# Taking 934 clears, and the waits for them, out from between GpSimd's indirect DMAs

## The chip, the cores and the metric

The kernel runs on one core of one Trainium2 chip. A core has five engines that run their own instruction streams: TensorE (PE), VectorE (DVE), ScalarE (ACT), GpSimd (POOL) and SyncE (SP). They meet only through semaphores. The metric is device time in microseconds (us) of one execution, as the median of the runs.

## The reference

Four graph layers, each followed by a layer norm, work on 100,000 nodes of 32 numbers and 25,000 edges that are sorted by `dst`. Cut to what matters:

```
x = norm(x + scatter_add(dst, message0(x[src], edge_weight, edge_attr_3)))      # layer 0
x = norm(x + mean of x and three hops of  segment_sum(w * x[src], dst))          # layer 1
x = norm(x + maximum(segment_max(mlp(x[src], x[dst], edge_attr_32), dst), x))    # layer 2
x = norm(x + (x + sum of attention messages over edges, by dst) @ W1 + b1)       # layer 3
```

Only nodes that are a `dst` get messages. The other nodes are norms and products of their own row alone. So the kernel keeps one row per edge for the `dst` side, and does the nodes in big chunks beside it.

## The kernel before

**Layout.** The 25,000 edges are padded to 25,088 and laid out as 128 partitions by T = 196 columns. A tile such as `A_dst` is [128, 196, 32]: one row of 32 numbers for each edge. Rows that are picked by an index come by an indirect DMA of one column: 128 indices, 128 rows. GpSimd issues them all, 1054 in the executed path, and nothing else issues one. The columns fall in 7 chunks of 28 (`GATHER_CHUNK`).

**GpSimd's stream, in order.** What it does is one straight line, written out by hand:

- 56 gathers of `x[src]` into `A_src` and 28 of `x[dst]` into `A_dst` (`in_x`). Here a helper `keep` paces them against VectorE's histogram. Nothing is cleared in front of them.
- 56 gathers from `pos_table` into `out_short` (columns of positions), 140 from `x_pos` into `A_src` (rows with the position appended), and 168 from `x` into `A_dst`. `x_pos` is a table that SyncE stores in 14 pieces; GpSimd waits for all of them (`x_stored`).
- the hops of layer 1: 60 gathers (`A_msg` from `table`, by `nxt_i`), 24 scatters to `edge_sums`, 22 gathers (by `idx_next`), 12 scatters, 22 gathers, 24 scatters, and 22 scatters from `A_tmp`. Each group waits for a table or for sums that VectorE makes out of the group before. VectorE does the node chunks (line 1495, line 2001 and others on `work`) between the hops, in an order that is fixed in its own stream.
- layer 2: 112 gathers (`work` from `table`), 16 for each of 7 windows; after each window VectorE moves rows into place with predicated copies (lines 2249 and 2253) and feeds the edge pipeline of TensorE and ScalarE.
- layer 3: 112 gathers (`A_msg` from `table`), again 16 for each of 7 windows, and then 196 scatters to `out` (line 880). The scatters come in 8 pieces of 20, six times 28, and 8 columns. Piece i waits for `final_ready` to reach i + 1, which VectorE's last multiplication of that piece (`A_dst<-A_dst,std`, line 1484) raises.

**The clear.** The helper `pause` (line 736 holds its memset) clears `gtmp[0:64]`, 64x64 numbers that nothing reads afterwards, raises the semaphore `cleared`, and makes GpSimd wait until that has arrived. It stands in front of 934 of the 1054 indirect DMAs. The other 120 go out one behind the other: the first 84 and the last 36 scatters to `out` (`if i < 6` leaves out pieces 6 and 7). Line 746 is the DMA in `gather`, lines 823 and 829 are those of the hops, line 880 is the scatter to `out`.

**VectorE's helpers.** Line 1484 is every elementwise operation of two tensors, line 1488 and line 1489 those of a tensor and scalars, line 1495 every reduction, line 1583 the running sums column by column (one scan for each of 32 features).

Of the kernel before, what the change touches and what calls it, by code (L numbers as in the profile page):

```python
# [10 lines left out]
T = -(-N_EDGES // P)  # L11
# [10 lines left out]
HEADS, HF = 2, 64  # L22
# [16 lines left out]
SLOTS_IN_WINDOW = 16  # L39
# [9 lines left out]
GATHER_CHUNK = 28  # L49
# [29 lines left out]
DST_FIRST = 1  # L79
# [9 lines left out]
def gnn_kernel(nc, x, src, dst, r_feat, rel, turned_attr, edge_weight, w1, b1, w2, b2,  # L89
# [12 lines left out]
    with ExitStack() as ctx:  # L102
# [3 lines left out]
        def sem(name):  # L106
            return ctx.enter_context(nc.semaphore(name))
# [5 lines left out]
        pos_table = dram("pos_table", (HI * P, 1))  # L113
# [157 lines left out]
        n_bank, seam_taken = sem("n_bank"), sem("seam_taken")  # L271
        n_var, n_std, n_z, n_zsq, n_out = sem("n_var"), sem("n_std"), sem("n_z"), sem("n_zsq"), sem("n_out")
        n_stored = [sem(f"n_stored_{s}") for s in range(SLOTS)]
        cleared = sem("cleared")
        mlp_in, maxima_taken = sem("mlp_in"), sem("maxima_taken")
        e_cat, e_turned, e_catT = sem("e_cat"), sem("e_turned"), sem("e_catT")
        e_h, e_hT, e_v, e_vused = sem("e_h"), sem("e_hT"), sem("e_v"), sem("e_vused")
# [419 lines left out]
        def _(pool):  # L697
# [32 lines left out]

            node_limit, edge_limit = pool.to_reg(N_NODES - 1), pool.to_reg(E_PAD - 1)

            def pause(tile):

                issued["cleared"] += 1
                pool.memset(tile, 0.0).then_inc(cleared, 1)  # L736
                pool.wait_ge(cleared, issued["cleared"])

            def gather(column, of, idx, limit, done, columns=range(T), keep=None, cleared_tile=None):

                for t in columns:
                    if keep:
                        keep()
                    if cleared_tile is not None:
                        pause(cleared_tile)
                    pool.indirect_dma_start(  # L746
                        out=column(t), out_offset=None, in_=of,
                        in_offset=bass.IndirectOffsetOnAxis(ap=idx[:, t:t + 1], axis=0),
                        bounds_check=limit, oob_is_err=False).then_inc(done(t), 16)

            pool.wait_ge(loaded_src, 48)
            pool.wait_ge(pads_ready, 2)
            issued = {"hist": 0, "cleared": 0}

            def keep_to_histogram():
                issued["hist"] += 1
# [2 lines left out]
                if k % 4 == 0 and need > 0:  # L759
                    pool.wait_ge(onehots_used, min(need, T // 2) + HIST_SLOTS)  # L760

            def gather_dst(columns, keep, cleared_tile=None):
                gather(lambda t: A_dst[:, t, :], x, dst_i, node_limit, lambda t: dst_rows[t // GATHER_CHUNK], columns,
                       keep=keep, cleared_tile=cleared_tile)

            plain = PLAIN * GATHER_CHUNK
            assert plain <= REST
# [3 lines left out]
            pool.wait_ge(zeros_stored, 80)  # L771
            gather_dst(range(DST_FIRST * GATHER_CHUNK), keep_to_histogram)
            pool.wait_ge(pos_stored, 32)
            gather(lambda t: pos_x[:, t:t + 1], pos_table, src_i, node_limit, lambda t: pos_rows, range(plain),
                   cleared_tile=gtmp[0:HF])

            for k in range(XP_SLOTS):
                pool.wait_ge(x_stored[k], 16 * len(range(k, D_CHUNKS + 1, XP_SLOTS)))
            gather(lambda t: src_wide[:, t, :], x_pos, src_i, node_limit, lambda t: src_rows[t // GATHER_CHUNK],
                   range(plain, T), cleared_tile=gtmp[0:HF])  # L780
            gather_dst(range(DST_FIRST * GATHER_CHUNK, T), None, gtmp[0:HF])

# [4 lines left out]
            def short_columns(move, done, columns, keep=None):  # L789

                for t in columns:
                    if keep and keep(t):
                        pool.wait_ge(n_out, keep(t))
                    pause(gtmp[0:HF])
                    move(t).then_inc(done, 16)
                if columns.stop < FEWEST:
                    return
                turns["short"] += 1
                with pool.If(n > FEWEST):
                    for t in range(FEWEST, FEW):  # L800
                        move(t).then_inc(more_done, 16)
                    pool.wait_ge(more_done, 16 * (FEW - FEWEST) * turns["short"])
                with pool.If(n > FEW):
                    pool.wait_ge(msg_cleared, 1)
                    for t in range(FEW, T):
                        move(t).then_inc(rest_done, 16)
                    pool.wait_ge(rest_done, 16 * (T - FEW) * turns["short"])
                pool.sem_inc(short_in, 1)

            def second_columns(move):  # L810

                turns["second"] += 1
                for t in range(FEWEST2):
                    pause(gtmp[0:HF])
                    move(t).then_inc(hop_done, 16)
                with pool.If(n2 > FEWEST2):
                    for t in range(FEWEST2, T):
                        move(t).then_inc(hop_rest, 16)
                    pool.wait_ge(hop_rest, 16 * (T - FEWEST2) * turns["second"])
                pool.sem_inc(short_in, 1)  # L820
# [36 lines left out]
            for k, of, order in zip((3, 4), compact, WINDOW_ORDER):  # L857
# [10 lines left out]
                for i, c in enumerate(order):  # L868
                    here = window_rows[k - 3][i % SLOTS]
                    if i >= SLOTS:  # L870
                        pool.wait_ge(here, 16 * SLOTS_IN_WINDOW * (i // SLOTS))
                    gather(lambda t: of[:, t, :], tables[k], pos_i, edge_limit, lambda t: here,
                           range(c * GATHER_CHUNK, c * GATHER_CHUNK + SLOTS_IN_WINDOW), cleared_tile=gtmp[0:HF])

            for i, c in enumerate(LAST_ORDER):
                pool.wait_ge(final_ready, i + 1)
                for t in range(T)[c] if isinstance(c, slice) else range(c * GATHER_CHUNK, (c + 1) * GATHER_CHUNK):
                    if i < 6:
                        pause(gtmp[0:HF])
                    pool.indirect_dma_start(  # L880
                        out=out, out_offset=bass.IndirectOffsetOnAxis(ap=out_i[:, t:t + 1], axis=0),
                        in_=A_dst[:, t, :], in_offset=None, bounds_check=node_limit,
# [1727 lines left out]
```

## Time and profile before

| | |
|---|---|
| median of 3 runs | 1860.24 us (1854.67 to 1861.78) |
| profiled execution, span from first to last instruction | 1863.2 us |
| GpSimd busy | 1400.9 us, 75% of the span |
| VectorE busy | 1344.3 us, 72% |
| TensorE busy, ScalarE busy | 729.3 us (39%), 488.0 us (26%) |
| DMA engines busy, mean of 16, most of the slices | 0.1 to 0.4, over 0.5 in five of 40 |

The span of the profiled execution is 3 us above the median of the runs, so a saving that is read from the trace can be taken off the median as it stands.

How to read the rows further down: a row of an instruction gives its start in us from the span's start, how long it took, and in brackets how long its engine had sat idle before it and what ended that. A GpSimd row of a DMA shows the time that GpSimd takes to put it out, not that of the data. Rows of groups give the busy time, the mean of one in ns, and the summed idle time in front.

### The profile page before, as it was taken

The numbers are of one execution on the slowest core, as the hardware profiler recorded it, in microseconds if no ns is written. First come the engines' busy times: TensorE is split into PE (matmuls) and PEld (weight loads), VectorE is DVE, ScalarE is ACT, GpSimd is POOL, SyncE is SP. The second block draws the span as 40 slices with busy tenths as digits, with TensorE's granted clock in tenths as the row PEclk, the third lists the DMA queues.
The fourth block names the chain that finished last, engine by engine and source line by source line (L and its number), as shares of the span: only waits on it lengthen the run. The fifth ranks groups of instructions, "written<-read, shape, count | busy, mean of one in ns | idle before, by whom it ended". The sixth has DMA issues, their size and how long they took to land.

```text
span 1863.2 us, 14783 instructions
## 1 busy us (share of the span) xinstructions
PE 729.3 (39%) x3676; PEld 546.2 (29%) x3676; DVE 1344.3 (72%) x2600; ACT 488.0 (26%) x1014; POOL 1400.9 (75%) x2019
## 2 busy tenths in 40 slices
PE   7912555541450003605337001456605656551400
PEld 3301222220220003605326001355505655551400
DVE  9955999986999645775755882478785999986400
ACT  7822311110110013522334200233302343342100
POOL 8878887888888885868878558884068888888776
PEclk9966778775785556867678555677757776665655
DMA  8165511111111101412222330000001111110000
GB/s 321 38 211 194 184 32 32 32 26 17 26 20 50 42 20 59 137 65 76 99 88 102 140 137 4 5 23 13 30 20 24 32 28 26 32 29 9 10 10 10
DMA packets 64097, 114.29 MB, mean 61 GB/s; under 512 B 27599, under 2 KB 48648, under 8 KB 63224
## 3 DMA queue, kind: packets, MB, share of 16 engines
q1 hardware_dynamic: 24304, 80.96, 12.0%
q0 software_dynamic: 33728, 12.79, 4.9%
q10 hardware_dynamic: 5960, 19.43, 2.8%
q8 instruction: 31, 0.51, 0.1%
q14 instruction: 74, 0.61, 0.1%
HBM read 61.66 MB, written 55.21 MB: 63 GB/s over the span
## 4 chain that ended last, share of the span: by engine, by line
POOL 75%; issue 17%; DVE 5%; PE 1%; DMA 1%; ACT 0%; POOLq 0%; SPq 0%; DVEq 0%
POOL A_dst L746 12%; POOL A_src L746 12%; POOL out L880 12%; POOL gtmp L736 9%; POOL work L746 8%; POOL A_msg L746 7%; POOL A_msg L823 7%; POOL edge_sums L829 5%; POOL out_short L746 3%; DVE A_dst L1484 1%; DVE stat L1495 1%; DVE work L2276 0%; DVE A_sum L1484 0%; PE bank L1388 0%; DVE A_dst L1492 0%
## 5 line engine op out<-in xcount | busy, mean ns | idle before, releaser
L746 POOL DMA_INDIRECT A_dst<-in_x,dst_i x196 | 224.3, 1144 | 57.4 <-POOL gtmp L736 39.1
L736 POOL MEMSET gtmp<- 64x64 f32 x934 | 156.5, 168 | 144.6 <-DMA table<-A_dst 110.9
L880 POOL DMA_INDIRECT out<-A_dst,out_i x196 | 217.9, 1112 | 59.7 <-POOL gtmp L736 34.3
L1495 DVE TENSOR_REDUCE work<-work 128x80 f32<-128x1280 f32 (+3 forms) x147 | 204.6, 1421 | 78.8 <-issue 50.2
L1310 PE MATMUL bank<-w2fold,work 128*128 128x384 f32 x392 | 183.1, 611 | 173.0 <-DVE work L1484 162.7
L746 POOL DMA_INDIRECT A_src<-x_pos,A_tmp x140 | 147.2, 1051 | 40.5 <-POOL gtmp L736 24.4
L746 POOL DMA_INDIRECT work<-table,pos_i x112 | 144.9, 1294 | 31.1 <-POOL gtmp L736 23.5
L1235 PE MATMUL bank<-ident,work 128*128 128x128 f32 (+1 forms) x294 | 63.4, 327 | 264.1 <-ACTq L995 139.2
L1310 PEld LDWEIGHTS bank<-w2fold,work 128*128 128x128 f32 x392 | 86.0, 237 | 269.5 <-issue 227.1
L746 POOL DMA_INDIRECT A_msg<-table,pos_i x112 | 139.0, 1241 | 32.4 <-POOL gtmp L736 16.5
L1484 DVE TENSOR_TENSOR work<-bank,work 128x384 f32<-128x384 f32 (+1 forms) x294 | 153.6, 590 | 0.2
L975 ACT ACTIVATE work<-A_tmp,b1col,w1col 65x256 f32<-65x256 f32 x98 | 58.3, 599 | 322.5 <-PE bank L1310 275.6
L1348 PE MATMUL bank<-nodes_w,small 128*128 128x128 f32 (+1 forms) x784 | 116.8, 306 | 63.2 <-ACT small L1006 59.2
L1348 PEld LDWEIGHTS bank<-nodes_w,small 128*128 128x128 f32 (+1 forms) x784 | 106.6, 215 | 72.9 <-ACT small L1006 67.1
L1235 PEld LDWEIGHTS bank<-ident,work 128*128 128x128 f32 (+1 forms) x294 | 41.8, 172 | 268.4 <-issue 165.1
L1235 PE MATMUL bank<-ident,end_col 128*32 128x128 f32 (+2 forms) x18 | 6.8, 379 | 271.1 <-DVE end_col L1540 239.1
L1235 PE MATMUL bank<-ident,A_tmp 128*65 128x128 f32 (+1 forms) x203 | 43.6, 355 | 123.7 <-DVE A_tmp L2369 113.8
L823 POOL DMA_INDIRECT A_msg<-table,nxt_i x60 | 74.4, 1239 | 17.9 <-POOL gtmp L736 9.3
L746 POOL DMA_INDIRECT A_src<-in_x,A_tmp x56 | 73.3, 1309 | 16.9 <-issue 16.9
L829 POOL DMA_INDIRECT edge_sums<-A_sum,out_short x60 | 72.0, 1200 | 17.9 <-POOL gtmp L736 12.2
L1235 PEld LDWEIGHTS bank<-ident,end_col 128*32 128x32 f32 (+2 forms) x18 | 1.7, 95 | 274.8 <-DVE end_col L1540 241.7
L1261 PE MATMUL bank<-A_msg,A_sum 128*128 128x392 f16 x392 | 80.0, 338 | 1.6 <-ACT A_sum L929 1.6
(396 smaller groups left out, 2335.5 us busy)
## 6 DMA issues: line engine op xcount, KB each, us to landing
work<-in_x SPq DMA_DIRECT2D x26, 960.0 KB
x_pos<-A_sum SPq DMA_DIRECT2D x13, 990.0 KB
out<-work ACTq DMA_DIRECT2D x13, 960.0 KB
A_tmp<-ew_turned_rows ACTq DMA_DIRECT2D x49, 130.0 KB
table<-A_dst SPq DMA_DIRECT2D x2, 3136.0 KB
edge_sums<-A_dst SPq DMA_DIRECT2D x2, 3136.0 KB
table<-A_dst SPq DMA_DIRECT2D x13, 448.0 KB
A_tmp<-in_edge_attr_2x SPq DMA_DIRECT2D x49, 112.0 KB
```

The costliest lines, as they stand in the source:

```text
L736: pool.memset(tile, 0.0).then_inc(cleared, 1)
L746: pool.indirect_dma_start(out=column(t), out_offset=None, in_=of, in_offset=bass.IndirectOffsetOnAxis(ap=idx[:, t:t + 1], axis=0), bounds_ ...
L823: return lambda t: pool.indirect_dma_start(out=column(t), out_offset=None, in_=of, in_offset=bass.IndirectOffsetOnAxis(ap=idx[:, t:t + 1], ...
L829: return lambda t: pool.indirect_dma_start(out=of, out_offset=bass.IndirectOffsetOnAxis(ap=idx[:, t:t + 1], axis=0), in_=column(t), in_off ...
L880: pool.indirect_dma_start(out=out, out_offset=bass.IndirectOffsetOnAxis(ap=out_i[:, t:t + 1], axis=0), in_=A_dst[:, t, :], in_offset=None, ...
L975: nc.scalar.activation(hidT[:, u % PAIRS_DEEP, :], ew_all[:, q % EW_SLOTS, slot * 2 * P:(slot + 1) * 2 * P], ACT.Relu, bias=b1col[:], scal ...
L1235: return nc.tensor.transpose(out_ap, in_ap, ident[0:n, 0:n])
L1261: last = nc.tensor.matmul(banks[6 + h][:, 0:half], lo_hot[:, 2 * slot + j, :], hi_hot[:, 2 * slot + j, h * half:(h + 1) * half], start=Fal ...
L1310: last = nc.tensor.matmul(banks[2 * (u % PAIRS_DEEP) + j][:, 0:PATHS], hid_rows[:, u % PAIRS_DEEP, j * P:(j + 1) * P], w2_rows[:], start=T ...
L1348: last = nc.tensor.matmul(node_products(i, w)[0:parts, k * P:(k + 1) * P], n_xT[:, s, k * parts:(k + 1) * parts], nodes_w[:, w * P:(w + 1) ...
L1484: return v.tensor_tensor(out=o, in0=a, in1=b, op=op)
L1495: return v.tensor_reduce(out=o, in_=a, axis=AX, op=op)
```

## The change

The helper `pause`, its semaphore and its counter are taken out, and every call of it. Nothing else is different: the same 1054 indirect DMAs in the same order, with the same other waits.

```
@@ gather
-            def pause(tile):
-
-                issued["cleared"] += 1
-                pool.memset(tile, 0.0).then_inc(cleared, 1)
-                pool.wait_ge(cleared, issued["cleared"])
-
-            def gather(column, of, idx, limit, done, columns=range(T), keep=None, cleared_tile=None):
+            def gather(column, of, idx, limit, done, columns=range(T), keep=None):
 
                 for t in columns:
                     if keep:
                         keep()
-                    if cleared_tile is not None:
-                        pause(cleared_tile)
                     pool.indirect_dma_start(
...
@@ hops: short_columns and second_columns
-                    pause(gtmp[0:HF])
                     move(t).then_inc(done, 16)
...
-                    pause(gtmp[0:HF])
                     move(t).then_inc(hop_done, 16)
...
@@ scatters to out
                 for t in range(T)[c] if isinstance(c, slice) else range(c * GATHER_CHUNK, (c + 1) * GATHER_CHUNK):
-                    if i < 6:
-                        pause(gtmp[0:HF])
                     pool.indirect_dma_start(
```

By place, 56 + 140 + 168 clears go before the first table of layer 1, 186 in the hops, 112 in layer 2, and 112 + 160 in layer 3: 934 in all.

## Rows read from the trace of the kernel before

**Rows 1.** Page, part 4: the chain that ended last, by engine.
```profile
POOL 75%; issue 17%; DVE 5%; PE 1%; DMA 1%; ACT 0%; POOLq 0%; SPq 0%; DVEq 0%
```

**Rows 2.** Groups of GpSimd: count, busy us, mean ns, idle before them and releaser.
```profile
L880 POOL DMA_INDIRECT out<-A_dst,out_i x196 | 217.9, 1112 | 59.7 <-POOL gtmp L736 34.3 <-issue 25.4
L736 POOL MEMSET gtmp<- 64x64 f32 x934 | 156.5, 168 | 144.6 <-DMA table<-A_dst 110.9 <-DMA table<-A_tmp 17.2 <-DVE A_sum L1484 12.6
L746 POOL DMA_INDIRECT A_src<-x_pos,A_tmp x140 | 147.2, 1051 | 40.5 <-POOL gtmp L736 24.4 <-issue 16.1
L746 POOL DMA_INDIRECT work<-table,pos_i x112 | 144.9, 1294 | 31.1 <-POOL gtmp L736 23.5 <-issue 7.6
...
L746 POOL DMA_INDIRECT A_src<-in_x,A_tmp x56 | 73.3, 1309 | 16.9 <-issue 16.9
```

**Rows 3.** Timeline of GpSimd, last clear and first DMAs without one.
```profile
1805.91 0.98 POOL L880 DMA_INDIRECT out<-A_dst,out_i  x1 [0.28 <-POOL gtmp L736]
1806.89 0.17 POOL L736 MEMSET gtmp<- 64x64 f32 x1
1807.33 0.98 POOL L880 DMA_INDIRECT out<-A_dst,out_i  x1 [0.28 <-POOL gtmp L736]
...
1810.04 0.98 POOL L880 DMA_INDIRECT out<-A_dst,out_i  x1 [0.30 <-issue]
1811.32 0.98 POOL L880 DMA_INDIRECT out<-A_dst,out_i  x1 [0.30 <-issue]
```

**Rows 4.** Timelines of VectorE and GpSimd where one waits for the other.
```profile
671.17 6.69 DVE L1484 TENSOR_TENSOR A_src<-A_src,small 128x6272 f32<-128x6272 f32 x1
...
671.51 7.23 POOL L746 DMA_INDIRECT A_dst<-in_x,dst_i  x1 [0.27 <-POOL gtmp L736]
...
569.01 14.85 DVE L1583 TENSOR_TENSOR_SCAN A_sum<-same,A_msg 128x196 f32<-128x196 f32 x32
...
571.80 12.93 POOL L746 DMA_INDIRECT A_dst<-in_x,dst_i  x1 [0.27 <-POOL gtmp L736]
...
89.42 1.35 POOL L746 DMA_INDIRECT A_src<-in_x,A_tmp  x1 [0.31 <-issue]
...
89.86 0.76 DVE L1488 TENSOR_SCALAR A_msg<-work,A_tmp 128x784 f16<-128x784 f16 x2
```

**Rows 5.** Waits of VectorE: for whom, us in total, times, longest.
```profile
DVE work L2253 <- DMA work<-table,pos_i: 73.3, 7, 17.3
...
DVE A_dst L1484 <- DMA A_dst<-in_x,dst_i: 48.1, 3, 26.8
...
DVE A_sum L1769 <- DMA A_src<-x_pos,A_tmp: 17.4, 1, 17.4
```

**Rows 6.** The tile x_pos: SyncE's stores, median ns of issue, first and last start.
```profile
L601 SPq DMA_DIRECT2D x_pos<-A_sum x14: 298/320/332, 117.3 to 207.6; - x14
```

**Rows 7.** Timeline of VectorE in the hops: its waits for GpSimd's data.
```profile
824.80 1.39 DVE L1583 TENSOR_TENSOR_SCAN A_sum<-small,A_msg 128x64 f32<-128x64 f32 x7 [5.86 <-DMA A_msg<-table,nxt_i]
...
975.62 1.49 DVE L1583 TENSOR_TENSOR_SCAN A_msg<-dst_f,A_msg 128x24 f32<-128x24 f32 x12 [5.92 <-POOLq L820]
...
1060.89 1.09 DVE L1492 SCALAR_TENSOR_TENSOR A_dst<-A_tmp,A_dst 128x896 f32<-128x896 f32 x1 [4.31 <-DMA A_tmp<-edge_sums]
```

**Rows 8.** Timeline of VectorE at the windows of layers 2 and 3.
```profile
1230.68 0.59 DVE L2253 COPY_PREDICATED work<-near_masks,work 128x384 f32<-128x384 uint8 x1 [2.86 <-DMA work<-table,pos_i]
...
1416.41 0.58 DVE L2253 COPY_PREDICATED A_msg<-near_masks,A_msg 128x384 f32<-128x384 uint8 x1 [17.43 <-DMA A_msg<-table,pos_i]
...
1442.67 0.58 DVE L2253 COPY_PREDICATED A_msg<-near_masks,A_msg 128x384 f32<-128x384 uint8 x1 [1.74 <-DMA A_msg<-table,pos_i]
```

**Rows 9.** Timelines: VectorE readies pieces 1 and 6, GpSimd starts piece 1.
```profile
1574.73 1.09 DVE L1484 TENSOR_TENSOR A_dst<-A_dst,std 128x896 f32<-128x896 f32 x1
...
1587.28 2.50 POOL L880 DMA_INDIRECT out<-A_dst,out_i  x1 [0.28 <-POOL gtmp L736]
...
1752.04 1.09 DVE L1484 TENSOR_TENSOR A_dst<-A_dst,std 128x896 f32<-128x896 f32 x1
```

More of the change, by code:

```diff
@@ L273, in gnn_kernel @@
         n_stored = [sem(f"n_stored_{s}") for s in range(SLOTS)]
-        cleared = sem("cleared")
         mlp_in, maxima_taken = sem("mlp_in"), sem("maxima_taken")
@@ L752, in _ @@
             pool.wait_ge(pads_ready, 2)
-            issued = {"hist": 0, "cleared": 0}
+            issued = {"hist": 0}
             def keep_to_histogram():
@@ L760, in keep_to_histogram, with gather_dst @@
                     pool.wait_ge(onehots_used, min(need, T // 2) + HIST_SLOTS)
-            def gather_dst(columns, keep, cleared_tile=None):
+            def gather_dst(columns, keep):
                 gather(lambda t: A_dst[:, t, :], x, dst_i, node_limit, lambda t: dst_rows[t // GATHER_CHUNK], columns,
-                       keep=keep, cleared_tile=cleared_tile)
+                       keep=keep)
             plain = PLAIN * GATHER_CHUNK
@@ L773, in _ @@
             pool.wait_ge(pos_stored, 32)
-            gather(lambda t: pos_x[:, t:t + 1], pos_table, src_i, node_limit, lambda t: pos_rows, range(plain),
-                   cleared_tile=gtmp[0:HF])
+            gather(lambda t: pos_x[:, t:t + 1], pos_table, src_i, node_limit, lambda t: pos_rows, range(plain))
             for k in range(XP_SLOTS):
@@ L779, in _ @@
             gather(lambda t: src_wide[:, t, :], x_pos, src_i, node_limit, lambda t: src_rows[t // GATHER_CHUNK],
-                   range(plain, T), cleared_tile=gtmp[0:HF])
-            gather_dst(range(DST_FIRST * GATHER_CHUNK, T), None, gtmp[0:HF])
+                   range(plain, T))
+            gather_dst(range(DST_FIRST * GATHER_CHUNK, T), None)
             pool.wait_ge(short_ready, 1)
@@ L872, in _ @@
                     gather(lambda t: of[:, t, :], tables[k], pos_i, edge_limit, lambda t: here,
-                           range(c * GATHER_CHUNK, c * GATHER_CHUNK + SLOTS_IN_WINDOW), cleared_tile=gtmp[0:HF])
+                           range(c * GATHER_CHUNK, c * GATHER_CHUNK + SLOTS_IN_WINDOW))
             for i, c in enumerate(LAST_ORDER):
```

## The prediction

> **What bounds the kernel now.** I read the chain that ended last first: 75% of it is GpSimd, 17% "issue" and 5% VectorE [rows 1]. The issue share is not somebody else's: it is the small idle time in front of GpSimd's own instructions. Second, the groups of GpSimd: 934 clears take 156.5 us (168 ns each), and the DMAs behind them have idle time of their own, 40.5 us for the 140 gathers from `x_pos` [rows 2]. Third, GpSimd's waits for others: the row of the clear shows 144.6 us, of which 110.9 us is for tables that VectorE has to finish [rows 2]. So GpSimd works in rows of DMAs without a rest, and at a few places hands over to VectorE. Fourth, VectorE's waits: 17.4, 48.1 and 73.3 us for GpSimd's gathers [rows 5]. Where the two wait for each other in turn, a faster GpSimd pays until VectorE has no wait left. That is the limit to look for at each place.
>
> **The price of one clear.** With a clear, a DMA costs GpSimd 0.98 + 0.17 + 0.28 us: the starts stand at 1805.91 and 1807.33, 1.42 us apart. Without one it is 0.98 + 0.30 us: 1810.04 to 1811.32, 1.28 us [rows 3]. So a DMA in the row does not lose its whole pause: 0.30 us of idle time stands between two DMAs anyway. The clear costs 0.14 us there, with VectorE idle. Over long rows it is a little more, since some handshakes come late: the 140 gathers from `x_pos` have 40.5 / 140 = 0.289 us of idle time, with the clear's 0.168 that is 0.457 us; the 56 from `in_x` without a clear have 16.9 / 56 = 0.302 us [rows 2]. The difference is 0.155 us. I take 0.155, because VectorE works beside most of the other rows as it does beside the `x_pos` gathers, and keep 0.14, from the rows at which it rests, as the low end. All 934 together are then 145 us (131 at the low end).
>
> **Time that a DMA is held by VectorE.** An undisturbed DMA takes 0.98 to 1.00 us. The means of 1.05 to 1.31 us of the groups [rows 2] come from VectorE. A subtraction of 6.69 us on two tiles in SBUF ran from 671.17; the DMA that began at 671.51 took 7.23 us and ended 0.88 us after it. Scans of 14.85 us in sum held one for 12.93 us. In the first stretch, where no clears stand, fp16 operations of VectorE hold each DMA to 1.35 us [rows 4]. What does the change do to this? A hold ends with VectorE's operation, whenever the DMA came. For short operations the DMA arrives at any phase, so the chance and the mean length of a hold per DMA stay as they are, and the 0.155 us is won in full. For a long one, the DMA that arrives earlier waits longer, and its 0.155 us is lost: two such operations of over 5 us are seen, too few to count. Bounds: nothing lost, or all of it lost at each held DMA. By the timeline about 250 of the 1054 DMAs, a quarter, took more than 1.05 us ([rows 4] shows three of them), so the far bound is a quarter of the saving. I take the first value: the group with few holds (mean 1.051) and the one with many (mean 1.294, idle 31.1 / 112 = 0.278 us) differ in the DMA's length and hardly in the gap [rows 2].
>
> *Beside the sum:* the Trainium skill (SBUF — State Buffer, "Who interferes with whom") says that a VectorE instruction with two SBUF inputs contends with a GpSimd instruction that reads SBUF, and not with one that only writes. The trace agrees on the first half (7.23 us beside 6.69 us) and a clear only writes, its mean being 168 ns throughout. The same page says that whoever starts first gets the ports for the whole instruction and the other blocks; by that, GpSimd without clears would hold VectorE more often. By that rule the sum would lose what VectorE is then held for; the trace has no VectorE operation that a DMA visibly lengthens, and the sum goes by the trace.
>
> **Place by place.**
>
> 1. Up to the first table (364 clears). 364 x 0.155 = 56 us. The gathers from `x_pos` cannot start before SyncE's last store, issued at 207.6 us [rows 6]; GpSimd would come after 56 x 0.155 = 8.7 us less than now, at about 210.7, which is 3 us after that issue. I take 1 us of loss. VectorE waits 17.4 us for the last `A_src` chunk and 48.1 us for chunks of `A_dst` [rows 5], 65.5 us in the order in which GpSimd gets ahead: enough for 55 us. Gain: 55 us.
>
> 2. The hops (186 clears). GpSimd would save 29 us. But VectorE does its node chunks between the hops in a fixed order, and waits for GpSimd for only 5.86, 5.92 and 4.31 us [rows 7]. What is late next is VectorE. Gain: the sum of these, 16 us. 13 us of GpSimd's saving is lost here.
>
> 3. Layer 2 (112 clears). 17 us. VectorE waits 73.3 us in seven waits for these windows [rows 5], the smallest being 2.86 us [rows 8]; 16 x 0.155 = 2.5 us comes off each window, so no wait is used up. The long wait for the next table that follows, most of the 110.9 us of [rows 2], only moves. Gain: 17 us.
>
> 4. Layer 3 (112 + 160 clears). 42 us, if GpSimd finds its pieces ready. Piece 1 is ready at 1575.8, and GpSimd comes to it with the clear in front of the DMA of 1587.28, at 1586.8 [rows 9], 11.0 us later. GpSimd would be 17.4 + 20 x 0.155 = 20.5 us earlier there. VectorE itself comes earlier by what it waits for gathers up to the third window, at most 3 x 2.5 = 7.4 us, of which 5.0 + 1.7 can be used [rows 8]. So GpSimd waits 20.5 - 11.0 - 6.7 = 2.8 us. Piece 6 is ready at 1753.1 [rows 9], and GpSimd starts it at 1810.04 now [rows 3], 57 us later: no limit. Gain: 39 us.
>
> Sum: 55 + 16 + 17 + 39 = 127 us. The profiled execution's span of 1863.2 becomes 1736 us, and the median of 1860.2 becomes **1733 us**. At 0.14 us per clear, places 1, 3 and 4 give 50 + 16 + 36 and the sum is 118, so 1742 us; with a quarter off places 1, 3 and 4 for held DMAs (115 / 4 = 29 us) it is 98 us, so 1762 us. At 0.17 us per clear, should the rest of the late handshakes be the clear's too, it would be 139 us, so 1721 us.
>
> **Rivals.**
>
> A. VectorE becomes the bound sooner. The waits of VectorE that I spend in place 1 are whole, but between them lies work that depends on TensorE and ScalarE. For it: in place 2 this is already so. Against it: 65.5 us of waits stand against 55 us. If place 1 gives only the last wait of VectorE, 26.8 us [rows 5], and layer 3 half, the sum is 27 + 16 + 17 + 20 = 80 us: 1780 us.
>
> B. Nothing is won, because the DMAs are paced by VectorE's operations. In the first stretch a DMA starts every 0.31 + 1.35 = 1.66 us although 1.30 us would do [rows 4]: held in step with VectorE. Against a clear of 0.14 us such a stretch is blind, since 1.44 us is also under 1.66. Against it: in rows 3, and in the group of mean 1.051, there is nothing of the kind. If all stretches are so, 1860 us.
>
> C. The unbroken row is worse against VectorE, and the kernel gets slower. With a clear, GpSimd leaves the read port alone for 0.44 us of 1.42; without, 0.30 of 1.28 [rows 3]. If the DMA now arrives where VectorE's operations follow each other closely, the hold is passed on from one operation to the next, as with the scans (12.93 us for one DMA) [rows 4]. The price: holds are the DMAs' time above 1.00 us. In the four groups of rows 2 that is 22 + 7 + 33 + 17 = 79 us for 504 DMAs, 0.16 us each, or 166 us for all 1054. The case decides once holds grow by over 127 us, that is from 0.16 to 0.28 us per DMA. If they double, it is 1860 - 127 + 166 = 1899 us. Against it: the only DMAs without a clear beside a busy VectorE, the first 56, are held to 1.31 us on average [rows 2], and VectorE has no operation on two SBUF tiles there. So the trace doesn't show the case that matters, and I cannot exclude it. A sentence apart: by the first-come rule of the Trainium skill's page named above (SBUF — State Buffer, "Who interferes with whom") VectorE would be the one that is blocked; the price would then fall on VectorE's operations, and the trace so far shows only GpSimd as the loser.
>
> **How the numbers follow.** The forecast (1710 to 1765) has 0.50, A with the quarter lost at held DMAs (1765 to 1850) 0.20, B (1851 to 1869) 0.08, and C 0.22, of which about a third ends under 1885. A difference of under 0.5%, 9 us, can't be told from no change here. So faster 0.70, same 0.08, slower 0.22. The range has to reach over A and B into C to leave out no more than 2 in 10: 1712 to 1885 us. The forecast's own range is 1710 to 1765.
>
> **What would show it.** In the profile after: rows of scatters to `out` 1.28 us apart from the first on, and no group of line 736. VectorE's waits for `A_src` and `A_dst` gathers near zero in place 1, the waits of rows 7 gone, the seven waits for `work` about 17 us less in sum, and the DMA groups' means unchanged within 0.03 us. Wrong by A: a new wait of GpSimd before the table of layer 1. Wrong by B: the idle gap gone into the DMAs' own time, one for one. Wrong by C: means of DMA_INDIRECT up by over 0.15 us, or VectorE's two-input operations longer than now (6.69 us for the subtraction).

## The result, and the profile after

| | before | after | ratio (95%) |
|---|---|---|---|
| first job (the prediction's result) | 1857.7 us (1854.7 to 1861.8, 4 runs) | 2256.5 us (2248.7 to 2302.9, 4 runs) | 1.213 [1.209, 1.216] |
| the same two kernels on chip 2, in the experiments | 1855.2 us (3 runs) | 1721.5 us (1717.8 and 1725.1) | 0.927 [0.921, 0.933] |

A run more than 1.5% above the fastest of the same kernel is left out of the ratios: 2302.9 us here, and 1930.9 us further down (e12).

The forecast was 1733 us, the range 1712 to 1885. The result is 2256 us, 21% slower than before and far outside it. But the second line is as real: the same program is 7% faster than before on another chip, 12 us from the forecast. Both have to be explained, first the slow one. Parts 1 and 4 of the page after (busy us and share of the span of each engine; the chain that ended last):

```profile
span 2254.7 us, 13849 instructions
...
PE 808.4 (36%) x3676; PEld 593.2 (26%) x3676; DVE 1345.7 (60%) x2600; ACT 486.1 (22%) x1014; POOL 1160.4 (51%) x1085
...
DVE 41%; another core or an unknown queue 21%; issue 18%; PE 12%; POOL 4%; ACT 4%; DMA 1%; ACTq 0%; DVEq 0%; POOLq 0%; PEld 0%; PEldq 0%
```

GpSimd has gone from 75% of the chain [rows 1] to 4%, and a fifth of the chain is in waits for which the profile finds no releaser. VectorE has no more to do: it is busy for 1345.7 us in 2254.7, and was for 1344.3 in 1863.2. Only TensorE is busier, 808.4 us for 729.3; its matmuls of the radial loop (`bank<-w2fold,work`) take 718 ns on average for 611, at a granted clock that is lower over the whole run (0.635 for 0.685). These 79 us do not make the 391.5 us that the span has grown by. GpSimd's own groups did what the forecast said (to compare with [rows 2]):

```profile
L737 POOL DMA_INDIRECT A_src<-x_pos,A_tmp x140 | 141.9, 1014 | 72.6 <-issue 42.3 <-DMA x_pos<-A_sum 30.3
L737 POOL DMA_INDIRECT work<-table,pos_i x112 | 137.9, 1231 | 124.5 <-issue 124.5
...
L811 POOL DMA_INDIRECT A_msg<-table,nxt_i x60 | 66.5, 1108 | 333.1 <-DMA table<-A_tmp 295.7 <-DVE work L1470 19.8 <-issue 17.7
```

The DMAs are no longer than before (1014 ns for 1051, 1231 for 1294). What is new is waits: 295.7 us for the first table, where it was 17.2 [rows 2]. The table is late because the work on the 49 column groups of edges that make it is late. Waits of ScalarE and VectorE, us in total, times, longest:

```profile
ACT work L961 <- remote: 317.9, 32, 11.3
...
DVE work L1470 <- remote: 219.7, 29, 9.6
```

"remote" stands where the profile finds nobody who raised the semaphore at that time. In the radial loop it is TensorE, and the timeline shows one turn of it (start us, duration, engine, what; idle before it in brackets):

```profile
324.06 0.60 ACT L961 ACTIVATE work<-A_tmp,b1col,w1col 65x256 f32<-65x256 f32 x1 [11.30 <-remote]
324.14 1.62 DVE L1470 TENSOR_TENSOR work<-bank,work 128x512 f32<-128x512 f32 x3
...
325.91 2.90 PE L1296 MATMUL bank<-w2fold,work 128*128 128x384 f32 x4 [9.15 <-DVE work L1470]
...
335.21 1.62 DVE L1470 TENSOR_TENSOR work<-bank,work 128x512 f32<-128x512 f32 x3 [9.45 <-remote]
335.27 0.60 ACT L961 ACTIVATE work<-A_tmp,b1col,w1col 65x256 f32<-65x256 f32 x1 [10.61 <-remote]
```

The four matmuls end at 325.91 + 2.90 = 328.81 (a modelled end). TensorE's semaphore goes up at 335.19 in the trace, 6.4 us later, and ScalarE and VectorE both go on at once. The other way there is no such delay: VectorE ends at 325.76, TensorE starts at 325.91. So four matmuls take 11.2 us, over and over, from about 281 us, 40 us into GpSimd's unbroken row (it begins at 240.8), until shortly after the row's end (646.9).

It is not the increment alone that is late. At the end of the same run TensorE has rows of weight loads (PEld) and matmuls; within a row they wait for no other engine, and only the last of seven or fourteen matmuls raises a semaphore. Beside the last scatters to `out`, of which the last starts at 2235.6 us, loads and matmuls start in turn, one every 1.40 us. When the scatters are over, seven such matmuls are through in 1.70 us:

```profile
2231.01 0.37 PE L1430 MATMUL bank<-gw,A_tmp 128*128 128x128 f32 x1 [2.43 <-issue]
2232.41 0.18 PEld L1221 LDWEIGHTS bank<-ident,A_msg 128*128 128x128 f32 x1 [2.50 <-issue]
2233.81 0.37 PE L1221 MATMUL bank<-ident,A_msg 128*128 128x128 f32 x1 [2.43 <-issue]
...
2247.95 1.70 PE L1221 MATMUL bank<-ident,A_msg 128*128 128x128 f32 x7
```

A turn of the radial loop has four loads and four matmuls, and 8 x 1.40 = 11.2 us is its length. So in this state each TensorE instruction seems to take its 1.40 us of something that they all pass through, whether it raises a semaphore or not; the four matmuls of the loop still start 0.6 to 0.8 us apart, and the delay shows in the increment of the last one.

### The profile page after: what moved, and what is told of

It reads as the page before. It is cut to its first block, busy times and chain, and to the rows that moved or that the text cites. A ratio compares the mean times of both kernels' runs of the same rounds, so it can differ in the third digit from the quotient of the medians.

```text
span 2254.7 us, 13849 instructions
## 1 busy us (share of the span) xinstructions
PE 808.4 (36%) x3676; PEld 593.2 (26%) x3676; DVE 1345.7 (60%) x2600; ACT 486.1 (22%) x1014; POOL 1160.4 (51%) x1085
## 4 chain that ended last, share of the span: by engine, by line
DVE 41%; another core or an unknown queue 21%; issue 18%; PE 12%; POOL 4%; ACT 4%; DMA 1%; ACTq 0%; DVEq 0%; POOLq 0%; PEld 0%; PEldq 0%
DVE work L1470 13%; DVE work L1481 6%; PE bank L1247 4%; POOL work L737 4%; PE bank L1221 3%; DVE A_dst L1470 2%; DVE stat L1481 1%; DVE A_tmp L1470 1%; PE bank L1334 1%; DVE A_sum L1569 1%; DVE r L1481 1%; DVE small L1481 1%; PE bank L1407 1%; DVE A_sum L1470 1%
## 5 line engine op out<-in xcount | busy, mean ns | idle before, releaser
L1296 PE MATMUL bank<-w2fold,work 128*128 128x384 f32 x392 | 222.8, 718 | 413.8 <-DVE work L1470 266.5
L1296 PEld LDWEIGHTS bank<-w2fold,work 128*128 128x128 f32 x392 | 98.7, 274 | 537.3 <-issue 509.7
L811 POOL DMA_INDIRECT A_msg<-table,nxt_i x60 | 66.5, 1108 | 333.1 <-DMA table<-A_tmp 295.7
L737 POOL DMA_INDIRECT A_dst<-in_x,dst_i x196 | 199.3, 1017 | 59.7 <-issue 59.7
L737 POOL DMA_INDIRECT work<-table,pos_i x112 | 137.9, 1231 | 124.5 <-issue 124.5
L1334 PE MATMUL bank<-nodes_w,small 128*128 128x128 f32 (+1 forms) x784 | 132.3, 333 | 165.0 <-ACT small L992 120.4
L737 POOL DMA_INDIRECT A_msg<-table,pos_i x112 | 118.0, 1053 | 120.6 <-issue 120.6
L737 POOL DMA_INDIRECT A_src<-x_pos,A_tmp x140 | 141.9, 1014 | 72.6 <-issue 42.3
L1334 PEld LDWEIGHTS bank<-nodes_w,small 128*128 128x128 f32 (+1 forms) x784 | 121.3, 241 | 175.7 <-ACT small L992 128.8
L1407 PE MATMUL bank<-gw,A_tmp 128*128 128x128 f32 x392 | 75.3, 356 | 52.8 <-issue 50.9
L1470 DVE TENSOR_TENSOR work<-bank,A_tmp 128x256 f32<-128x256 f32 x49 | 20.5, 419 | 116.1 <-ACT A_tmp L1118 65.9
L1407 PEld LDWEIGHTS bank<-gw,A_tmp 128*128 128x128 f32 x392 | 70.4, 269 | 54.1 <-issue 51.9
```

The lines of the kernel that those rows point to most:

```text
L737: pool.indirect_dma_start(out=column(t), out_offset=None, in_=of, in_offset=bass.IndirectOffsetOnAxis(ap=idx[:, t:t + 1], axis=0), bounds_ ...
L811: return lambda t: pool.indirect_dma_start(out=column(t), out_offset=None, in_=of, in_offset=bass.IndirectOffsetOnAxis(ap=idx[:, t:t + 1], ...
L1296: last = nc.tensor.matmul(banks[2 * (u % PAIRS_DEEP) + j][:, 0:PATHS], hid_rows[:, u % PAIRS_DEEP, j * P:(j + 1) * P], w2_rows[:], start=T ...
L1334: last = nc.tensor.matmul(node_products(i, w)[0:parts, k * P:(k + 1) * P], n_xT[:, s, k * parts:(k + 1) * parts], nodes_w[:, w * P:(w + 1) ...
L1407: last = nc.tensor.matmul(banks[2 + slot][:, j * P:(j + 1) * P], cat3_rows[:, slot, j * P:(j + 1) * P], gw2_rows[:], start=True, stop=True)
L1470: return v.tensor_tensor(out=o, in0=a, in1=b, op=op)
```

## Experiments: the break in the row

My first theory was that GpSimd must stop now and then for the others' semaphore increments to get through. Four kernels thin out the clears or shorten them. The edits stand in `pause`:

```diff
 e1: all 934 clears, each 64x4 instead of 64x64, still waited for at once
+                j = issued["cleared"] % 16
                 issued["cleared"] += 1
-                pool.memset(tile, 0.0).then_inc(cleared, 1)
+                pool.memset(tile[:, 4 * j:4 * j + 4], 0.0).then_inc(cleared, 1)
                 pool.wait_ge(cleared, issued["cleared"])
 e2: as e1, but the wait is for the clear 15 places back
+                if issued["cleared"] >= 16:
+                    pool.wait_ge(cleared, issued["cleared"] - 15)
...
-                pool.wait_ge(cleared, issued["cleared"])
 e3, e4, e5: the full clear and its wait at every 4th, 16th, 64th place
+                issued["asked"] = issued.get("asked", 0) + 1
+                if issued["asked"] % 4 != 1:
+                    return
```

> Every clear is cut to a sixteenth of the dead tile (64 rows of 4 floats), the next sixteenth each time, and GpSimd waits for it at once, as in the kernel before. Theory Q (what the clears buy is the wait: with it GpSimd's instruction stream never runs ahead of the engine, without it semaphore increments of TensorE, VectorE and ScalarE come late): nothing changes, 1840 to 1870 us. Theory R (the clears buy a slower rate of DMAs and a share of idle time; the time of one clear itself counts): the clear is shorter, the rate a little higher, so something between the kernel before and the kernel after, 1870 to 2000 us.

> The same 934 clears of 64 rows of 4 floats, but ahead of each GpSimd waits for the clear 15 places back, which is long done, and not for the one just issued: the same instructions, and only the distance of the wait is other. Theory Q (the wait at once holds GpSimd's instruction stream back): as slow as the kernel after, 2150 to 2300 us, the first table's last edge rows at about 940 us, and TensorE's increments in the radial loop between 281 and 640 us some 6 us behind the modelled end. Theory R (the rate of the DMAs, the time the clears take): the clears are there, so as with the waits, 1840 to 1900 us.

> The full clear with its wait stands at every fourth of the 934 places only. Theory Q: the stream is let ahead by at most 4 DMAs, some 5 us; if the lateness grows with how far it is ahead, this is nearly the kernel before with three quarters of the clears' time given back: 1770 to 1860 us. Theory R: the mean cycle of a DMA is 1.35 us where the kernel after has 1.316 and the kernel before 1.505 to 1.623, so three quarters of the loss is there: 2050 to 2250 us.

> The full clear with its wait stands at every sixteenth place only. Theory Q with a lateness that needs the whole run-ahead (some 14 DMAs in the kernel after): 1800 to 2000 us; with a lateness that needs only a few DMAs unbroken: nearly as after, 2150 to 2260 us. Theory R: as after, 2200 to 2260 us. Beside the run at every fourth place it shows how the loss grows with the length of the unbroken row.

Measured on chip 14, before 1858.9 us: 1784.8, 1727.7, 1744.7 and 1720.4 us. None of the four lies in a range that either theory had given, the second least of all: with no wait at once and a cycle of 1.34 us it should have been slow by the one and 1840 us by the other.

```diff
 e6: no clear; a look at a semaphore that has long been up
+                if issued["cleared"] % 16 == 1:
+                    pool.wait_ge(pads_ready, 2)
 e7: one column cleared, no semaphore, no wait
+                if issued["cleared"] % 16 == 1:
+                    pool.memset(tile[:, j:j + 1], 0.0)
 e8: as e4, but none after the 364 places up to the first table
+                if issued["asked"] % 16 != 1 or issued["asked"] > 364:
+                    return
```

> The full clear with its wait stands at every sixty-fourth of the 934 places only (15 are left). Theory S (what costs is a long row of GpSimd's DMAs with none of its other instructions in it; in the kernel after the lateness of TensorE's increments sets in some 40 to 50 us, 30 to 40 DMAs, after such a row has begun): rows of 64 are a half late, so between the run at every sixteenth place (1720 us) and the kernel after (2256 us): 1850 to 2100 us. Theory U (any break in the long rows of 308 and 112 DMAs is enough, since the lateness needs a row of over 64): 1710 to 1740 us.

> No clear at all; at every sixteenth place GpSimd waits for a semaphore that has stood at its value since the start, so the wait never lasts. Theory V (GpSimd's instruction stream must stop to look at a semaphore now and then): 1710 to 1740 us. Theory W (the engine itself must run something that is not a DMA): as the kernel after, 2200 to 2300 us.

> At every sixteenth place GpSimd clears one column of the dead tile, another each time, raises no semaphore for it and waits for nothing. Theory W (an instruction that runs on the engine between the DMAs is what matters): 1710 to 1740 us. Theory V (the look at a semaphore is what matters): as the kernel after, 2200 to 2300 us.

> The full clear with its wait stands at every sixteenth of the first 364 places (up to the first table) and nowhere behind. In the kernel after, GpSimd starts on the first table at 942.6 us and ends 1294 us later; with a clear at every sixteenth place everywhere these are 654.2 and 1054 us. If the loss behind the first table is made there, by its own unbroken rows of 112 and fewer: 654 + 1294, about 1950 us. If it is made in the front part alone (something late that is carried on): 1710 to 1760 us.

Measured on chip 4, before 1856.1 us: 1706.8, 1715.7, 1704.2 and 1720.4 us. All fast, whatever stood in the row. e6 and e7 were to exclude each other and did not, so the theory that they were to refine was wrong. What no run had yet asked was whether the kernel after itself is slow there.

## Experiments: the same kernel on other chips

e9 is the kernel after, unchanged. e10 is the kernel before with `return` as the body of `pause`; e11 is the kernel after and e12 the kernel before, unchanged.

> The kernel after, once more, beside the kernel before on the chip of the next run. It is there as the yardstick: eight kernels that keep between none and 934 of the breaks in GpSimd's rows take 1704 to 1785 us. If the slowness belongs to the program: 2240 to 2310 us. If it belonged to a chip or a moment: 1690 to 1730 us.

> The kernel before with an empty body for the clear: GpSimd issues exactly what it issues in the kernel after, and what is left of the clears is their semaphore, which keeps its place in the list and is never used; so the 60-odd semaphores made behind it keep the numbers that they have in the kernel before. Theory X (the unbroken row of DMAs up to the first table makes the loss, and one break in 64 is enough to avoid it): as the kernel after, 2200 to 2310 us. Theory Y (GpSimd's row has nothing to do with it; the semaphores or the program have moved): 1690 to 1730 us.

On chip 2: 1721.5 and 1727.1 us. The slowness does not belong to the program alone. Whether the numbering of the semaphores has a part in it can't be read from a chip on which nothing is slow; e13 and e16 below answer it, since they keep the numbers of the kernel before and are slow. The page of e9, parts 1 and 4:

```profile
span 1723.4 us, 13849 instructions
...
POOL 26%; DVE 13%; issue 9%; PE 4%; ACT 2%; DMA 1%; ACTq 0%; POOLq 0%; DVEq 0%
```

In the radial loop of e9, TensorE's end and ScalarE's start belong together: 329.93 + 3.06 = 332.99, and 333.08.

```profile
329.93 3.06 PE L1296 MATMUL bank<-w2fold,work 128*128 128x384 f32 x8 [1.51 <-DVE work L1470]
...
333.08 0.60 ACT L961 ACTIVATE work<-A_tmp,b1col,w1col 65x256 f32<-65x256 f32 x1 [0.93 <-PE bank L1296]
```

> The kernel after a third time, on whatever chip the job gets. Theory C (the 2256 us belong to the chip or the moment of the first job, in which semaphore increments pile up under GpSimd's unbroken rows: its trace has 57 of them recorded per 40 us from 280 to 640 us, where the fast run of the same kernel has some 600): 1715 to 1730 us on most chips, and 2240 to 2310 us if such a chip comes up again. Theory D (the kernel after has two levels of its own on every chip): either level within the runs of one chip.

> The kernel before, for its trace on this chip. Theory C: on a chip where the kernel after is fast, 650 to 900 recorded increments per 40 us between 80 and 200 us, where the first job's chip shows 400, 79 and 299; its time 1855 to 1862 us all the same, since its cycle of 1.5 to 1.6 us leaves the pile time to go. If the first trace's low counts belong to the program: 400, 79, 299 again.

The job got chip 1: the kernel after 2326.9 us, the kernel before 1868.1 us (3 runs; the two of e12 took 1868.9 and 1930.9). Theory C holds, ratio 1.246 [1.242, 1.249], and theory D does not: no chip shows both levels. I call the chips kind A (2, 4, 10, 14) and kind B (the first job's, whose number is not on record and which may be one of the others, 1 and 7). The kernel after itself ran on three: 1721 us on chip 2, 2256 us in the first job, 2327 us on chip 1. The others are put down to a kind by their relatives and by the sign that follows. The kernel before shows hardly anything of it: 1855 to 1861 us on kind A, 1858 to 1868 on kind B.

The page does carry a sign of the kind, though. Part 6 gives the time from a DMA's issue to its landing. The stores of `x_pos` in the kernel after, first job, then in e9:

```profile
x_pos<-A_sum SPq DMA_DIRECT2D x13, 990.0 KB
```

```profile
x_pos<-A_sum SPq DMA_DIRECT2D x13, 990.0 KB, 6.6
```

On kind B that number is missing in every trace, in the first profile of the kernel before and in e12 too, since many increments of the semaphores have no record; on kind A all traces have it. Counted over 40 us, the recorded increments of all semaphores:

```
                     120-160 us   mean of 280-640 us
kind B  before             79         493
kind B  e12 (before)       72         452
kind B  after              69          58
kind B  e11 (after)        64          57
kind A  e9 (after)        769         548
```

So on kind B something is at its limit from some 120 us on, in either kernel. The kernel before gets out of it at about 180 us, with a GpSimd DMA (16 increments each) every 1.51 us. The kernel after does not, with one every 1.32 us, and its own trace shows what lets go: in the 20 us from 200 us on, 37 increments are recorded; then GpSimd stands for 30.3 us, until 240.8, and from 220 to 260 us there are 205 and 191 in 20 us; from 260 to 280 us, in the new row, there are 83, and by 281 us TensorE is late again.

## Experiments: rate or wait

I say that a kernel falls where TensorE becomes late as above and the time goes over 2100 us, and that it holds where the time stays under 1900. The kernel before, which holds on kind B, has a lower rate and also a wait at each clear. Three pairs tell these apart, e13 with e14, e15 with e16, e17 with e18. The first two ran on chips of kind B.

```diff
 e13: as e2      e14 and e18: as e1      e16: as e3, with % 2
 e15: four clears at each place, each waited for 15 clears late
+                for _ in range(4):
+                    j = issued["cleared"] % 16
+                    if issued["cleared"] >= 16:
+                        pool.wait_ge(cleared, issued["cleared"] - 15)
+                    issued["cleared"] += 1
+                    pool.memset(tile[:, 4 * j:4 * j + 4], 0.0).then_inc(cleared, 1)
 e17: as e1, in the first 364 places only
```

> Clears of 64 rows of 4 floats, waited for 15 places late, on whatever chip the job gets; which kind it is shows in the semaphore increments recorded from 120 to 160 us, some 770 on the fast kind and 60 to 80 on the slow kind. On the fast kind 1728 us again. On the slow kind, theory E (the rate alone decides; increments pile up when a DMA of 16 comes every 1.32 us and not when one comes every 1.5 us): its cycle of 1.34 us is nearly that of the kernel after, 2150 to 2330 us. Theory F (anything between the DMAs lets the increments through): 1720 to 1780 us.

> The same clears of 64 rows of 4 floats, each waited for at once, on the same chip. On the fast kind 1785 us again. On the slow kind, theory E: its cycle of 1.43 us lies between the two known ones (1.32 slow, 1.51 not), so either 1785 to 1800 us, if the turn is below it, or 1850 to 2150 us; in any case less than with the wait 15 places late. Theory F: 1785 to 1800 us.

> Four clears of 64 rows of 4 floats at each place (3736 in all), each waited for 15 clears late, so that no wait stops GpSimd at once; four clears of 0.12 us fill the gap between two DMAs and bring the cycle to an estimated 1.5 to 1.55 us. On the fast kind of chip 1830 to 1900 us. On the slow kind, theory E (the rate decides): 1850 to 1920 us and over 300 recorded increments per 40 us from 280 to 640 us. Theory G (the wait at once decides, by stopping GpSimd until the increment is through): 2150 us or more, with 60 to 100 increments per 40 us.

> The full clear, waited for at once, at every second place (467 left): a mean cycle of 1.41 us before the first table. On the fast kind 1775 to 1800 us. On the slow kind, theory E: 1.41 us lies at the turn (1.43 holds, 1.34 falls), so 1790 to 2100 us; theory G: 1780 to 1820 us.

Measured (cycle: us from one start to the next, over the 140 gathers from `x_pos` and the 168 of `A_dst` behind them; count: recorded increments per 40 us, 280 to 640 us):

| kind B | waits at once | cycle `x_pos` | cycle `A_dst` | count | time, us | before there |
|---|---|---|---|---|---|---|
| after (first job) | none | 1.319 | 1.320 | 58 | 2256 | 1857.7 |
| e13, chip 7 | none | 1.409 | 1.414 | 101 | 2199.9 | 1866.8 |
| e16, chip 1 | every 2nd | 1.403 | 1.420 | 90 | 2101.1 | 1866.5 |
| e14, chip 7 | every | 1.446 | 1.496 | 304 | 1829.4 | 1866.8 |
| e15, chip 1 | none | 1.454 | 1.504 | 276 | 1893.0 | 1866.5 |
| e12, before, chip 1 | every | 1.513 | 1.627 | 452 | 1868.9 | 1868.1 |

By the mean cycle the runs part in two: up to 1.42 us they fall, from 1.45 us on they hold. A wait at once is not enough by itself (e16 has 467 of them and falls), and it is not needed (e15 has none and holds). That the rate alone decides is not shown, though. Where VectorE holds no DMA, e16 and e15, on the same chip, have the same pace: e16 1.44 and 1.31 us by turns, 1.37 on average, and e15 1.37:

```profile
299.44 1.00 POOL L749 DMA_INDIRECT A_src<-x_pos,A_tmp  x1 [0.30 <-issue]
...
300.88 1.00 POOL L749 DMA_INDIRECT A_src<-x_pos,A_tmp  x1 [0.27 <-issue]
302.19 1.00 POOL L749 DMA_INDIRECT A_src<-x_pos,A_tmp  x1 [0.30 <-issue]
```

```profile
299.33 1.00 POOL L749 DMA_INDIRECT A_src<-x_pos,A_tmp  x1 [0.15 <-issue]
...
300.70 1.00 POOL L749 DMA_INDIRECT A_src<-x_pos,A_tmp  x1 [0.15 <-issue]
```

What lifts e15's mean is more time under VectorE's holds (its DMAs take 1.072 us on average in the two rows, e16's 1.023), which are fewer where VectorE stands because the kernel has fallen, and eight pauses of 1.64 to 1.90 us between two DMAs, where nearly all others have 0.37. So the mean cycle is in part an effect of holding or falling, and 1.42 to 1.45 us is where the means of six runs part, not a threshold. Besides, e15's wait reaches back 15 clears, which is less than four DMAs or 5.5 us, and TensorE is 6.4 us late in a fallen run: e15 can be stopped by its own late clears (the profile counts 17 waits for a clear in the whole run, 9.9 us), and whether it would hold without that, no run tells. (In e13 the wait reaches back 15 DMAs. It has 0.380 us from the end of one DMA to the start of the next, where e2 with the same edit has 0.305 on kind A; late increments of its clears would do that, but it is not shown that they do.)

Of the expectations, e14's 1829.4 us lies between its two ranges, e15's count of 276 is under the 300, and e16's 2101.1 us is 1 us over its range.

GpSimd's waits for the first table (the group also holds one short wait), e16 and then e14:

```profile
POOL gtmp L739 <- DMA table<-A_tmp: 201.8, 2, 189.4
```

```profile
POOL gtmp L737 <- DMA table<-A_tmp: 28.9, 2, 17.3
```

Not every increment seems to weigh the same: with those of its clears e15 has 20 / 1.454 = 13.8 per us from GpSimd and its DMAs, more than the kernel after with 12.1, and does not fall. Whether the clears' increments weigh nothing is open: e15 takes 64 us more than e14 at nearly the same cycle (on another chip, but with the kernel before at 1866.5 and 1866.8 us there). Nor is "holds" a clean line: e15 takes 26 us more than the kernel before on the same chip (ratio 1.014 [1.000, 1.029]), at a faster cycle, and e14 falls for a moment at its very end. Its last 36 scatters have no clear between them; they begin at 1776.1 us, and from 1785.7 to 1813.1 us TensorE's loads and matmuls start 1.40 us apart, as in the kernel after. Such steps, 1.38 to 1.42 us apart with at most one of the two raising or awaiting a semaphore, are in the traces of kind B: 53 in the kernel after, 41 in e11, 32 in e13, 24 in e15, 22 in e14, 9 in e16, none in the two traces of the kernel before (first job and e12), where TensorE has finished before its last 36 scatters begin. On kind A no trace has one.

> Clears of 64 rows of 4 floats, each waited for at once, in the first 364 places only; behind the first table GpSimd's DMAs follow each other unbroken, as in the kernel after. On the fast kind of chip 1745 to 1775 us (1785 us less the clears behind the table). On the slow kind: if the rows behind the table fall by themselves, the first table's last rows come at 695 to 700 us as with short clears everywhere, and the part behind takes nearly what it takes in the kernel after (1294 us from the start of GpSimd's first table row; 1124 us with short clears everywhere): 1900 to 2000 us. If the fall there is a sequel of the one in front: 1760 to 1830 us.

> The short clears at all 934 places, once more, with an interval. On the fast kind of chip 1783 to 1788 us, ratio 0.96; on the slow kind 1825 to 1835 us, ratio 0.98: faster than the kernel before on either, by both theories of the cause. Anything over 1855 us would say that it is too near the turn.

This job got chip 10, kind A, before 1861.2 us: 1749.4 and 1802.3 us, ratios 0.940 [0.936, 0.944] and 0.967 [0.965, 0.970]. So whether the rows behind the first table cost as much by themselves on kind B stays open (that an unbroken row can fall by itself, after a run that held, e14's end shows), and e18 missed its own expectation by 15 us: its 168 gathers for `A_dst` went at 1.577 us, against 1.495 in e1. What stands is that the short clears (e1, e14, e18) are faster than the kernel before on both kinds: 0.960 [0.957, 0.963], 0.980 [0.977, 0.984] and 0.967.

## Why the prediction was wrong, step by step

The places begin with GpSimd's first DMAs of the first table, of layer 2 and of layer 3, and the last ends with the span: 720.85, 1088.79, 1362.32 and 1863.2 us in the first trace of the kernel before, 664.83, 1008.22, 1257.77 and 1723.4 in e9. The gain of each, in us (before less after; in the kernel after of the first job the places begin at 942.60, 1413.77 and 1672.29 us, and the span is 2254.7):

| place | forecast | e9, kind A | after, kind B |
|---|---|---|---|
| 1, to the first table | 55 | 56.0 | -221.8 |
| 2, the hops | 16 | 24.6 | -103.2 |
| 3, layer 2 | 17 | 24.0 | +15.0 |
| 4, layer 3 and the tail | 39 | 35.2 | -81.5 |
| sum | 127 | 139.8 | -391.5 |

- **The price of one clear** (0.155 us) was right. e9 has 1.334 us a cycle in the `x_pos` row where the kernel before has 1.509, so 0.175 us; over all 364 clears of place 1 it is 56.0 / 364 = 0.154 us.
- **Place 1** came out to 1 us on kind A. VectorE's waits were used in part: for `A_dst` 48.1 us [rows 5] became 23.9, for `A_src` 17.4 became 5.7. That is 36 us; from where VectorE has the other 20 I have not traced, since the profile of before is of kind B and e9 of kind A, where TensorE's handshakes are quicker too. The loss at the stores of `x_pos` did not come: their last issue moved from 207.6 [rows 6] to 187.8 us on kind A. On kind B it moved to 236.9, and GpSimd stood for 30.3 us.
- **Place 2** was sized too low: 24 us for 16. The step added up VectorE's three waits in [rows 7]; GpSimd gained 27.0 us up to the end of the hops' last row, of the 29 that its clears cost, and only 2.5 came back in front of layer 2 (32.7 us from that end to the first DMA before, 35.2 in e9). So VectorE was not what came late next.
- **Place 3** gave 24 us for 17: the DMAs got shorter besides (1218 ns on average, 1294 before). **Place 4**: GpSimd's wait at piece 1, 2.8 us in the forecast, is 12.5 us.
- **The DMAs held by VectorE** were rightly left alone. On kind A one of 6.80 us stands beside a subtraction of 6.69 us, where there were 7.23 beside 6.69 [rows 4]. Rival C's price, longer holds (means up by over 0.15 us), appears on neither kind: on kind A the means of GpSimd's groups moved by -0.10 to +0.03 us, on kind B none rose by more than 0.001 us. The subtraction is not longer either, so the first-come rule of the Trainium skill (SBUF — State Buffer, "Who interferes with whom"), by which VectorE would be blocked more often, does not show here.
- **The step that failed** is none of the four terms but what stood under all of them. The prediction took GpSimd and VectorE waiting for each other in turn as "the limit to look for at each place", and put the effect of the denser DMAs on TensorE and ScalarE at nothing, without a reason: rival A names their work only as something that VectorE might wait for. On kind B TensorE's handshakes depend on how densely GpSimd's DMAs come. With the cycle from 1.51 down to 1.32 us each TensorE instruction costs 1.40 us, a turn of the radial loop 11.2 us, and GpSimd waits 295.7 us for the first table where it waited 17.2. The chance of 0.22 for "slower" was given to a mechanism that had no part in it, rival C, and the range's end at 1885 us was taken from that rival. That the kernel after comes within 12 us of the forecast on kind A bears out the sum, not this step.

Could the trace of before have shown it? Only in part. Its page had no landing times, and its recorded increments fell to 79 in 40 us once (120 to 160 us), where a chip of kind A has 769. Beside a trace of kind A this would have said that something is at its limit; which way a change of 10% in rate would go could not be read from it.

**What stays open.** What saturates. The runs show that it goes with GpSimd's DMAs coming densely (their increments and their packets come in step, and no run parts the two), that TensorE's increments reach the others some 6.4 us late under it, and that records of increments are missing at the same time. Two readings are at hand. Either the increments themselves queue up, or the writing of records does and holds the engines back. The steps of 1.40 us between TensorE instructions that raise no semaphore speak against increments alone, and for something that each instruction passes through; a record is written for each of them (both traces of the kernel after have all 13849), but that it is the record is argued, not shown. Every execution timed here was also recorded, so no run tells the two apart for good, and on the second reading an execution without records might not be slow at all. The Trainium skill allows for the second: by NOTIFIC — the notification-queue block, "7.1 Overflow: three behaviours, one of which stalls the engine", a full ring can lose new records or, if so set, stall their producer, and the block's inner pipeline holds producers back rather than lose a record. That records of increments are lost is seen here; which of the two the delay is, is not. Open too is why chips differ, and whether the kind stays with a chip: chip 1 came up twice and was kind B both times, every other chip that is on record by its number came up in one job.

## What to carry to other kernels

An instruction that "does nothing" in front of a long row of DMAs can be the brake that keeps the row under a limit that no engine's busy time shows and that only some chips have; before taking it out, look at the rate it leaves behind (here a DMA of 16 increments every 1.32 us fell and one every 1.45 us held), and at every engine's handshakes, not only at those of the two engines in the chain. Shorten it first: clears of a sixteenth of the size won 2 to 4% on both kinds of chip, while none at all won 7% on one and lost 21 to 25% on the other. And when a result makes no sense against its own trace, run the unchanged kernel again on another chip before explaining it; e1 to e8 could only be understood once e9 had run.

## What the runs showed of the hardware

- The same program takes 1721 us on one chip and 2256 or 2327 us on others, with repeats within 0.5% on each but for one of 2302.9 us, while the kernel before has medians of 1855 to 1868 us on all of them.
- With GpSimd's indirect DMAs 1.32 us apart, TensorE's semaphore increments arrive 6.4 us after the end of the matmul on kind B; VectorE's reach TensorE within 0.2 us in the same stretch. TensorE's weight loads and matmuls start 1.40 us apart there when they follow each other, also those that raise no semaphore, and are back at their usual distance 9 us after the start of the last DMA (2235.6 and 2244.5 us).
- On kind A a short clear that is not waited for at once costs nothing next to a DMA: 1.338 us a cycle in e2, 1.334 in e9 without any. It fits into the 0.30 us that lie between two DMAs anyway. Waited for at once it costs 0.10 us (1.434 in e1), in full size 0.175 (1.509 in the kernel before, whose trace is of kind B). Where VectorE holds no DMA the three cycles are 1.30, 1.39 and 1.44 us.
- Four clears that are not waited for at once still cost less than one full clear that is: 1.454 us a cycle (e15) against 1.513 (e12), on the same chip.
